# Attention and int8 feed-forward on one core: the third and fourth key tile's probabilities added by accumulating DMAs

## The reference

```python
q = (x @ Wq)...; k = (x @ Wk)...; v = (x @ Wv)...         # k, v repeated for the 4 query heads of each
scores = jnp.einsum('bhqd,bhkd->bhqk', q, k) / sqrt(HEAD_DIM)
attn = jax.nn.softmax(scores, axis=-1)
out = jnp.einsum('bhqk,bhkd->bhqd', attn, v)
x = _layernorm(x + out.reshape(B, S, 512) @ Wo)

x_q, w_q = round(x / x_scale), round(weight / w_scale)     # clipped to int8, a scale for each row
y = (x_q @ w_q.T) * x_scale * w_scale + bias
x = _layernorm(x + y)
```

## Time and profile before

| | |
|---|---|
| runs | 869.13, 876.8 and 1778.66 us, median 876.8 |
| span of the profiled execution | 865.9 us |
| median above that span | 10.9 us |
| lowest run above that span | 3.2 us |
| TensorE's mean granted clock in it | 0.959 of full speed |
| moved by DMA | 62.16 MB, 72 GB/s on average |
| read from HBM, written to it | 20.71 MB, 8.39 MB |

### The profile page before, as it was taken

How to read it: one execution, slowest core, us unless ns; L and a number is a source line. 1 busy time by engine, 2 the same in 40 slices (tenths; PEclk the granted TensorE clock), 3 DMA queues, 4 the chain that set the end, 5 groups by cost and what they waited for, 6 DMA issues and landing times.

```text
span 865.9 us, 14242 instructions
## 1 busy us (share of the span) xinstructions
PE 775.2 (90%) x3723; PEld 439.2 (51%) x3752; DVE 700.6 (81%) x1131; ACT 493.8 (57%) x904; POOL 609.5 (70%) x672
## 2 busy tenths in 40 slices
PE   7688999999899988999899997999989998899864
PEld 5444544565456544565446653466545654344432
DVE  5689678788887896888988887778988889789666
ACT  4155566555666664665565555566656665557644
POOL 3375687588776785877875886748788678777934
PEclk9799999999999998999999998899999999999995
DMA  8521133132222322132131322212231322300001
GB/s 230 150 83 37 40 73 99 31 80 63 82 79 69 77 77 75 41 96 77 50 109 36 78 63 81 83 44 74 69 103 46 83 78 62 98 25 27 30 21 48
DMA packets 40924, 62.16 MB, mean 72 GB/s; under 512 B 10385, under 2 KB 12433, under 8 KB 40833
## 3 DMA queue, kind: packets, MB, share of 16 engines
q1 hardware_dynamic: 39488, 57.38, 24.5%
q0 software_dynamic: 1344, 3.74, 1.7%
HBM read 20.71 MB, written 8.39 MB: 34 GB/s over the span
## 4 chain that ended last, share of the span: by engine, by line
PE 34%; issue 23%; DVE 17%; POOL 16%; POOLq 5%; ACT 2%; DMA 1%; SPq 0%; DVEq 0%; ACTq 0%
POOL prob_sum L1000 14%; PE s_bank L367 7%; PE st_bank L376 7%; DVE row_max L778 6%; PE front_bank L322 6%; PE o_bank L391 6%; PE tail_bank L322 4%; POOLq L1009 3%; PE z_bank L405 3%; DVE o_norm L802 2%; DVE o_norm L796 1%; POOLq L1007 1%; DMA probs<-in_L_attn_Wv 1%; PE front_bank L329 1%; POOL rs L1010 1%
## 5 line engine op out<-in xcount | busy, mean ns | idle before, releaser
L778 DVE TENSOR_REDUCE row_max<-s_bank 128x1 f32<-128x512 f32 x512 | 341.6, 684 | 90.8 <-PE s_bank L367 89.0
L604 ACT ACTIVATE probs<-st_bank 128x512 f32<-128x512 f32 x512 | 293.1, 595 | 192.4 <-PE st_bank L376 187.1
L1000 POOL TENSOR_TENSOR prob_sum<-prob_sum,probs 128x512 f32<-128x512 f32 x248 | 346.1, 1426 | 7.8 <-ACT probs L604 3.9
L376 PE MATMUL st_bank<-q_stack,k_stack 98*128 98x512 f32 x512 | 231.2, 453 | 16.4 <-issue 6.6
L367 PE MATMUL s_bank<-k_stack,q_stack 96*128 96x512 f32 x512 | 213.1, 419 | 25.2 <-DVE row_max L778 24.4
L1000 POOL TENSOR_TENSOR prob_sum<-probs 128x512 f32<-128x512 f32 x128 | 169.4, 1349 | 74.8 <-PE z_bank L405 55.3
L376 PEld LDWEIGHTS st_bank<-q_stack,k_stack 98*128 98x128 f32 x512 | 98.0, 192 | 120.4 <-ACT probs L604 80.2
L391 PE MATMUL o_bank<-probs,v_tok 128*32 128x512 f32 x1024 | 140.7, 623 | 0.7 <-ACT probs L604 0.7
L367 PEld LDWEIGHTS s_bank<-k_stack,q_stack 96*128 96x128 f32 x512 | 99.3, 194 | 65.8 <-DVE row_max L778 42.3
L1005 POOL TENSOR_TENSOR rs<-mv,small 128x1 f32<-128x1 f32 x64 | 12.6, 196 | 123.7 <-DVE mv L822 123.7
L322 PE MATMUL tail_bank<-wo_hi,o_hi 128*128 128x512 f32 x112 | 46.1, 412 | 6.3 <-issue 6.3
(11 more groups left out here) (192 smaller groups left out, 1056.9 us busy)
## 6 DMA issues: line engine op xcount, KB each, us to landing
q_stack<-q_parts SPq DMA_DIRECT2D x357, 64.0 KB, 2.0
x_tok<-in_L_attn_x SPq DMA_DIRECT2D x36, 256.0 KB, 3.6
y_sb<-in_L_attn_x SPq DMA_DIRECT2D x28, 256.0 KB, 2.6
out<-u_sb SPq DMA_DIRECT2D x28, 256.0 KB, 2.2
k_stack<-k_parts SPq DMA_DIRECT2D x90, 64.0 KB, 2.0
probs<-in_L_attn_Wq SPq DMA_DIRECT2D x1, 1024.0 KB, 7.6
o_norm<-in_L_attn_Wo POOLq DMA_DIRECT2D x4, 256.0 KB, 8.2
q_stack<-neg_max SPq DMA_DIRECT2D x64, 8.0 KB, 1.9
```

The source lines that it names most:

```text
L376: nc.tensor.matmul(st_bank[:, j % 2, :], k_stack[0:STACK_M, p, j, kt * P:(kt + 1) * P], q_stack[0:STACK_M, i, j, :], start=True, stop=True ...
L604: nc.scalar.activation(probs[:, kt, j, :], st_bank[:, j % 2, :], ACT.Exp, scale=SCALE).then_inc(exp_done, 1)
L778: nc.vector.tensor_reduce(row_max[:, i % 2, j * QT + qt:j * QT + qt + 1], s_bank[:, qt % 2, :], AX_X, ALU.max).then_inc(max_done, 1)
L1000: nc.gpsimd.tensor_tensor(prob_sum[:, j, :], first, probs[:, kt, j, :], ALU.add).then_inc(sum_done, 1)
```

## The change

GpSimd adds only the first two key tiles (four additions for a group, `pair_done`). The third and the fourth are each added to `prob_sum` by one DMA of 1 MB from SBUF to SBUF that POOL issues, with addition as its accumulate operation (`gather_probs`). Such a DMA counts `gathered` up by 16 when it has landed, so a group has 32 (`GATHERED`). `sums` waits for `gathered` in place of `sum_done`. POOL issues the first of the two when all four first additions and all four exponentials of the third key tile are done; the second when the first has landed and the fourth key tile's exponentials are done. Ahead of each it drains and does an addition of one column (`gather_mark`), which carries the wait for the exponentials. The last group of all is as before: `sums` takes two tiles from `probs`.

```diff
--- before.py
+++ after.py
@@ -162,7 +162,7 @@
     STACK = 3 * HEAD
     STACK_M = STACK + 2
     STACKED = 16 * 3 * NKV
-    ADDS = NKV * (QT - 1)
+    GATHERED = 16 * (QT - 2)
     PASSES = 3 * KC
     assert (D, S, GROUPS, QT, KC) == (512, 512, 4, 4, 4) and B % 2 == 0
 
@@ -206,6 +206,7 @@
         rs1, rs2 = sb("rs1", [P, QT, 4]), sb("rs2", [P, QT, 4])
         small = sb("small", [P, 3])
         stack_mark = sb("stack_mark", [P, 3])
+        gather_mark = sb("gather_mark", [P, 1])
         freed_mark = sb("freed_mark", [P, 6])
         x_scale = sb("x_scale", [P, QT, 3])
 
@@ -252,7 +253,8 @@
         mt_done, mh_done, ml_done = sem("mt_done"), sem("mh_done"), sem("ml_done")
         m_stacked = [sem(f"m_stacked{i}") for i in range(GROUPS)]
         st_done, exp_done, pv_done, o_read = sem("st_done"), sem("exp_done"), sem("pv_done"), sem("o_read")
-        sum_done, z_done, ln_done, inv_done = sem("sum_done"), sem("z_done"), sem("ln_done"), sem("inv_done")
+        pair_done, gathered = sem("pair_done"), sem("gathered")
+        z_done, ln_done, inv_done = sem("z_done"), sem("ln_done"), sem("inv_done")
         correct_done, scaled_done, norm_done = sem("correct_done"), sem("scaled_done"), sem("norm_done")
         o_hi_done, o_lo_done, wo_done = sem("o_hi_done"), sem("o_lo_done"), sem("wo_done")
         last_hi_done, last_lo_done = sem("last_hi_done"), sem("last_lo_done")
@@ -398,7 +400,10 @@
                 pe.wait_ge(ml_done, b * GROUPS + i + 2 if not (is_last(b) and i == GROUPS - 1) else B * GROUPS)
 
                 apart = is_last(b) and i == GROUPS - 1
-                pe.wait_ge(sum_done, (b * GROUPS + i) * ADDS + ADDS - (2 * NKV if apart else 0))
+                if apart:
+                    pe.wait_ge(pair_done, B * GROUPS * NKV)
+                else:
+                    pe.wait_ge(gathered, (b * GROUPS + i + 1) * GATHERED)
                 addends = (prob_sum[:], probs[:, QT - 2], probs[:, QT - 1]) if apart else (prob_sum[:],)
                 for n, addend in enumerate(addends):
                     for j in range(NKV):
@@ -595,7 +600,10 @@
                 if j == 0:
 
                     wait(act, pv_done, b * STEPS + u // NKV - 3)
-                    wait(act, sum_done, (b * GROUPS + i - 1) * ADDS + (NKV, NKV, 2 * NKV, 3 * NKV)[kt])
+                    if kt < 2:
+                        wait(act, pair_done, (b * GROUPS + i) * NKV)
+                    else:
+                        wait(act, gathered, (b * GROUPS + i - 1) * GATHERED + 16 * (kt - 1))
                     if isinstance(b, int) and b == 0 and i == 0:
 
                         act.wait_ge(*((wq_lo_done, GROUPS), (wkv_lo_done, 2), (q_stacked[1], STACKED),
@@ -990,14 +998,21 @@
             def add_probs(b, s, j):
 
                 i, kt = divmod(s, QT)
-                if kt == 1:
-                    wait(pool, z_done, b * GROUPS + i)
-                    first = probs[:, 0, j, :]
+                wait(pool, z_done, b * GROUPS + i)
+                pool.wait_ge(exp_done, b * UNITS + s * NKV + j + 1)
+                nc.gpsimd.tensor_tensor(prob_sum[:, j, :], probs[:, 0, j, :], probs[:, kt, j, :], ALU.add).then_inc(pair_done, 1)
+
+            def gather_probs(b, s):
+
+                i, kt = divmod(s, QT)
+                pool.drain()
+                if kt == 2:
+                    pool.wait_ge(pair_done, (b * GROUPS + i + 1) * NKV)
                 else:
-                    pool.wait_ge(sum_done, (b * GROUPS + i) * ADDS + (kt - 2) * NKV + j + 1)
-                    first = prob_sum[:, j, :]
-                pool.wait_ge(exp_done, b * UNITS + s * NKV + j + 1)
-                nc.gpsimd.tensor_tensor(prob_sum[:, j, :], first, probs[:, kt, j, :], ALU.add).then_inc(sum_done, 1)
+                    pool.wait_ge(gathered, (b * GROUPS + i) * GATHERED + 16 * (kt - 2))
+                pool.wait_ge(exp_done, b * UNITS + (s + 1) * NKV)
+                nc.gpsimd.tensor_tensor(gather_mark[:], small[:, 0:1], small[:, 0:1], ALU.add)
+                pool.dma_start(prob_sum[:], probs[:, kt, :, :], accum_op=ALU.add).then_inc(gathered, 16)
 
             def inv_std(n, t, mv, mv_done, rs, done):
 
@@ -1021,8 +1036,10 @@
 
                     pb, ps = (b, s - 1) if s else (b - 1, STEPS - 1)
 
-                    if ps % QT > 0 and (s > 0 or tail) and (front or s == 0 or ps < STEPS - 2):
+                    if ps % QT == 1 and (s > 0 or tail):
                         add_probs(pb, ps, j)
+                    if ps % QT > 1 and j == 0 and (s > 0 or tail) and (front or s == 0 or ps < STEPS - 2):
+                        gather_probs(pb, ps)
 
             nc.gpsimd.memset(ident[:], 0.0).then_inc(ident_set, 1)
             pool.wait_ge(ident_set, 1)
```

## The result

The change makes the kernel slower: 1040.96 us (1035.92 to 1047.78, four runs) against 873.87, a ratio of 1.1956 [1.1898, 1.2014]. One of the four runs of the kernel before took 1778.66 us; the ratio leaves it out (the median of the other three is 870.93). The forecast was 940 us: the right sign, inside the range, but 63 us more where 167 were measured between the medians. The profiled execution has a span of 1040.2 us, against 865.9.

What follows compares the result with a forecast made beforehand. TensorE, 90% busy, was taken as the bound, held by GpSimd ahead of `sums`. 865.9 + 92 (late sums) - 9 (absorbed) - 20 (relief) = 929; those 63 us more on the 876.8 median gave 940 us, range 862 to 1070.

Steps and rivals of the forecast that it cites:

- relief: Fewer GpSimd adds: 13 us from VectorE's shorter two-SBUF-input operations, 7 us from ScalarE's waits for `rs`; together 20 us gained.
- The length of a transfer: Issue to landing of one 1 MB accumulating DMA into `prob_sum`: 8.0 us, from two passes; ends 4.8 and 10.6.
- The step ahead of an issue: On GpSimd before each accumulating DMA, drain, marker and semaphore hop: 0.6 us, between 0.3 and 1.2.
- The chain's term: Two serial transfers make `sums` late by 11.9 us per four groups; over 31 groups 92 us.
- a tenth: Share of the 92 us loss absorbed as engines behind catch up with TensorE's idle time: 9 us.
- The first step that failed: 64 KB stack copies on the shared DMA engines land in 2.0 us with units of room; doubling them costs nothing.
- The second: Layer-norm scalings behind GpSimd's wait for the first landing cost nothing, as their inputs come later; cover gone above 11 us.
- (a): Rival: accumulating transfer as fast as a plain one, 4.8 us; `sums` never late, 20 us gained, 857 us; chance 0.13.
- (b): Rival: transfer of 6.0 to 7.1 us; `sums` loses 4 to 38 us against 20 gained, within 2%; chance 0.12.
- (c): Rival: reads and write don't overlap or packets queue, transfer 10.6 us; 208 us more, 1085 us; chance 0.17.

Runs made afterwards that it cites:

- a_sem: Changed kernel with semaphore waits in place of the two drains in GpSimd's layer-norm operations (`inv_std`): 993.19 us, ratio 1.1426 to the kernel before.
- b_sem: Kernel before the change, with semaphore waits in place of the two drains in `inv_std`: 861.13 us, ratio 0.9887.
- a_small_sem: Changed kernel with semaphores for `inv_std`'s drains and each accumulating transfer cut to 64 KB, rest left out of the sums: 834.77 us, ratio 0.9571.
- a_free_sem: Changed kernel with semaphores for `inv_std`'s drains; 1 MB accumulating transfers go to memory nothing reads, `sums` waits only for first adds: 940.73 us, ratio 1.0798.
- a_plain_sem: Changed kernel with semaphores for `inv_std`'s drains and plain 1 MB copies over `prob_sum` in place of accumulating transfers: 870.69 us, ratio 0.9995.

## Why the prediction was right in direction and short in size

**The sum of the runs.** Along one order of the edits: 869.6 (before, in a_sem's job); -8.5 for the drains (b_sem 861.1); -26.3 relief (a_small_sem 834.8); +105.9 for the bytes alone (a_free_sem 940.7); +52.5 for the chain that `sums` waits for (a_sem 993.2); +47.8 for the drains on top (1041.0). That is +171.4. The terms come from different jobs, whose medians of the kernel before lie within 2 us of each other (869.6 to 871.7). The parts overlap: the drains cost 48 us with the chain and 76 without it, so another order would give other terms.

**The length of a transfer** was right, 7.9 us for 8.0, as two passes at the plain rate; a plain copy 4.9 for 4.8. The Trainium skill ("Collectives: The Full Stack", section "The bandwidth ceiling: the fold count and why AG ≠ RS ≠ AR") says, of the adding transfers in a ring of cores, that the second source read halves the rate; 7.9 against 4.9 us fits that, once some 2 us are taken off as fixed (5.9 to 2.9). The step ahead of an issue is 0.7 to 0.8 us (0.6).

**The relief** was right in mechanism and a little small, 26 us for 20. Of these 20, 7 were for ScalarE's waits for `rs`, and those hardly move, from 22.6 + 10.3 us in b_sem to 17.6 + 10.5 in a_small_sem; how the rest divides between VectorE's shorter operations and GpSimd's shorter queue is not shown. GpSimd is busy 331.7 us for 300.

**The chain's term** ("31/4 x 11.9 = 92 us", less 9) had the right size for what it describes. From the moment when a group's third tile and first additions are ready to the start of `sums`, the 31 groups have 442.6 us before, 555.1 in a_sem (597.6 in the changed kernel), summed over their timelines: 112.5 more. But 25.5 of them are also there in a_free_sem (468.1), where `sums` does not wait for the transfers, and the 87.0 on top of that become only 52.5 us of time. So, as an estimate from these sums, some 35 us are absorbed, two fifths where "a tenth" was taken; that engines which the traffic holds up would have waited anyway is argued, not shown. Against that, the matmuls came back from each long gap at the lower clock, 49 us more busy time over the kernel, which the prediction had at nothing.

**The first step that failed** is "The stack copies of 64 KB share the DMA engines; they land in 2.0 us and have units of room, so doubling them costs nothing." A median is not what holds an in-order queue. It is still 2.0 us after; but 88 of the 357 copies of q take more than 3 us, where 7 did, and up to 7.6; the maxima's copies reach 7.0 us, x's loads 8.2 in the median, and a_free_sem puts the traffic at 106 us, the largest term of all. It was named as what would make the prediction wrong, and given no price.

**The second** is "The layer-norm scalings stand in POOL's queue behind the wait for the first landing, but their own inputs come later". That looked at the wait that the change adds and not at the drains that `inv_std` has had all along. They hold for the landing of either transfer, so being past the wait was no cover; ScalarE, and then TensorE, waited behind them: 48 us (a_sem).

**The rivals.** (a) and (b) rested on the length alone; a_plain_sem has (a)'s length and is not faster, so its 20 us of gain would not have come with 1 MB moved at the plain rate. (c)'s 10.6 us is refuted by the landings, although its 1085 us lies closer to the result than 940.

**Open.** The runs don't separate how much of the traffic's 106 us is SP issuing late, how much landing late, and how much the lower granted clock (0.962 in a_small_sem, 0.910 in a_free_sem) that follows. The chain alone, without the bytes, was not tried. Plain copies of the same size cost at most 36 us (a_plain_sem over a_small_sem) with a chain, and accumulating ones 106 without, at the same count of 62; so it is not the count of transfers. Whether it is the time of the engines in all or the length of the single transfer is not separated, since both grow together; why an 8 KB copy waits so long among quarters too is not shown.

## What to carry to other kernels

Before bulk transfers are put beside small ones that an in-order queue waits for, price the longest landing of the small ones (behind one large transfer) and not their median; taking the large ones off the path by giving them an unused destination measures that cost directly (106 us here). Look for every drain behind the place where an engine issues a transfer: on GpSimd it waited for the landing here, and a semaphore between the dependent operations did the same work 48 us faster. A gap of five microseconds on TensorE cost more than itself here, since the granted clock came back at 0.50, so the longer matmuls belong in the sum beside the wait. And before a transfer is cut into pieces, price the issues: four of 1376 ns on GpSimd in place of one of 892.

## What was not expected of the hardware

- A GpSimd drain holds for the landing of transfers that GpSimd issued: up to 7.77 us, with 140.9 us of idle time behind it at 46 places; 45.2 with plain copies. Even where GpSimd issues none in the loop, replacing 128 drains by semaphores gained 8.5 us (b_sem).
- Cutting 1 MB of accumulation into four transfers of 256 KB makes it dearer, 43.4% against 36.9% of the engines and 221.3 against 55.3 us of issues on GpSimd. Beside the pieces the longest landing of the maxima falls only from 7.3 to 5.9 us, that of the stores from 9.1 to 4.0.
- 62 transfers of 1 MB from SBUF to SBUF, for which `sums` does not wait, lengthened the kernel by 106 us. The Trainium skill ("SBUF — State Buffer", section "Who interferes with whom") says that a DMA never contends with a compute engine; for the duration of instructions no row here speaks against it (L802's counterpart takes 883 ns beside these transfers), but the transfers that the engines wait for pay for it.
